# A ResNet-style block and a spatial attention on Trainium2: the end of the work ("drain") written out anew

## The reference, cut to what matters

```
x = x + L0(gn(x))
    # L0: r = relu(sum over 4 groups of lambda * bn2(conv3x3(sign(relu(bn1(conv3x3(sign(v)))))))  + v),  v = gn(x)
x = x + L1(gn(x))
    # L1: mid = v * m                       v = gn(x), m = mask resized to 28x28
    #     atten = sigmoid(conv7x7([mean over channels of mid, max over channels of mid, m]))
    #     out = mid * atten
    #     relu(5 * ((out - mean) * rsqrt(var + eps) * gamma + beta))     mean, var of each image and channel
```

## Time and profile before

| | us |
|---|---|
| median of 3 runs (258.95 to 261.13) | 260.57 |
| the profiled execution | 262.13 |
| its span, first to last instruction | 260.3 |
| PE busy, share of the span | 226.2, 87% |
| DVE | 224.4, 86% |
| ACT | 187.2, 72% |
| POOL | 169.4, 65% |
| mean granted clock of PE | 0.951 |

### The profile page before, as it was taken

One profiled execution on the slowest core, in us unless ns is written; L12 is line 12 of the kernel. 1 busy time (PEld: TensorE's weight loads), 2 busy tenths in 40 slices (PEclk: granted clock), 3 DMA queues, 4 the chain that ended last, 5 costly groups with the idle time before them and its releaser, 6 DMA issues.

```text
span 260.3 us, 7041 instructions
## 1 busy us (share of the span) xinstructions
PE 226.2 (87%) x2693; PEld 145.3 (56%) x2693; DVE 224.4 (86%) x535; ACT 187.2 (72%) x228; POOL 169.4 (65%) x242
## 2 busy tenths in 40 slices
PE   8789887979999999998999999999999998577640
PEld 3356544555666566655665666557565666335630
DVE  4899899899999999999999999999899997565181
ACT  3966777878878987797979897989798863351311
POOL 4458121553526557498958797979697868889842
PEclk9999999999999999999999999999999999779555
DMA  6999604202010602241225122521342044141114
GB/s 201 373 289 400 236 13 125 70 0 64 3 63 16 176 0 64 83 107 65 64 73 178 62 64 74 180 75 56 105 146 95 31 140 152 58 154 62 62 62 185
DMA packets 11975, 28.81 MB, mean 111 GB/s; under 512 B 2230, under 2 KB 3383, under 8 KB 11943
## 3 DMA queue, kind: packets, MB, share of 16 engines
q1 hardware_dynamic: 11797, 28.37, 33.4%
q10 hardware_dynamic: 146, 0.01, 0.0%
HBM read 21.76 MB, written 6.61 MB: 109 GB/s over the span
## 4 chain that ended last, share of the span: by engine, by line
DVE 41%; PE 22%; issue 11%; POOL 10%; DMA 7%; ACT 6%; SPq 1%; POOLq 0%; DVEq 0%
DVE bnst L646 9%; DVE big L702 7%; PE big L1006 6%; PE big L985 6%; DVE RD L725 5%; POOL X L435 4%; DVE acc L733 3%; DVE S L705 3%; PE small L1046 3%; PE big L1079 3%; DVE gate L699 3%; DMA o<-in_w 2%; PE small L1060 2%; POOL o L415 2%; DVE red L755 2%
## 5 line engine op out<-in xcount | busy, mean ns | idle before, releaser
L1006 PE MATMUL big<-S,w2t 64*64 64x392 f16 x1152 | 55.3, 332 | 5.0 <-DVE S L705 4.9
L985 PE MATMUL big<-E,w1t 64*128 64x392 f16 x576 | 54.5, 331 | 1.3 <-DVE w1t L800 1.1
L1006 PEld LDWEIGHTS big<-S,w2t 64*64 64x64 f16 x1152 | 30.7, 106 | 24.7 <-DVE S L705 9.0
L985 PEld LDWEIGHTS big<-E,w1t 64*128 64x128 f16 x576 | 25.5, 94 | 23.6 <-issue 5.4
L1025 PE MATMUL big<-RD,wa 128*64 128x392 f16 x384 | 35.0, 330 | 3.2 <-issue 3.2
L1046 PE MATMUL small<-cs,o 128*112 128x130 f32 x224 | 33.6, 291 | 4.7 <-POOL o L415 2.2
L415 POOL TENSOR_TENSOR o<-o,mask_b 128x784 f32<-128x784 f32 x15 | 27.8, 1853 | 13.0 <-ACT o L569 10.3
L435 POOL TENSOR_TENSOR X<-X,acc 128x784 f32<-128x784 f32 x15 | 27.7, 1849 | 11.6 <-ACT acc L563 11.6
L1046 PEld LDWEIGHTS small<-cs,o 128*112 128x112 f32 x224 | 26.8, 179 | 15.0 <-issue 8.1
L646 DVE BATCH_NORM_STATS2 bnst<-X 128x6 f32<-128x392 f32 x64 | 32.9, 555 | 1.9 <-POOL X L435 1.1
L705 DVE SCALAR_TENSOR_TENSOR S<-big,thr,gate 128x784 f16<-128x784 f32 (+1 forms) x32 | 32.3, 1011 | 1.1
(11 more groups left out here) (130 smaller groups left out, 354.7 us busy)
## 6 DMA issues: line engine op xcount, KB each, us to landing
X<-in_x SPq DMA_DIRECT2D x16, 392.0 KB, 11.8
mask_b<-mask_rows SPq DMA_DIRECT2D x32, 196.0 KB, 4.0
out<-o SPq DMA_DIRECT2D x16, 392.0 KB, 2.4
att_b<-attention_rows SPq DMA_DIRECT2D x28, 196.0 KB, 3.7
o<-in_w SPq DMA_DIRECT2D x3, 576.0 KB, 7.2
o<-in_masks SPq DMA_DIRECT2D x1, 512.0 KB, 10.2
band<-in_band SPq DMA_DIRECT2D x1, 441.0 KB, 9.7
cs<-in_cst SPq DMA_DIRECT2D x1, 399.0 KB, 9.3
```

Of the source, the lines that this page charges most:

```text
L985: mm = pe.matmul(acc[:, LOW + HALF * hh:LOW + HALF * (hh + 1)], w1t[64 * hh:64 * hh + 64, q, s, :], window(RH * hh, s // 3, s % 3, E[64 * ...
L1006: mm = pe.matmul(acc[64 * q:64 * q + 64, LOW + HALF * r:LOW + HALF * (r + 1)], w2t[64 * r:64 * r + 64, s, 64 * q:64 * q + 64], window(RH * ...
```

## The change

The loops of the four engines run to k = 14. Step 15 and the drain are written out:

- The last pair's L0 is finished by halves of 392 columns in PSUM: `mix(15, 0)` stands ahead of `group_2(14)` and `turn(13, 1)`, `mix(15, 1)` behind `turn(13, 2)`; `finish_half` (DVE), `relu_halves` (ACT) and `add_half` (DVE, with its `bn_stats`) work in place in `big1`. `X[:, 15]` is not written, the last sum reads the PSUM.
- `normalise2(15)` is gone. u is made from the sums as (x - mean) * mask by `make_u_part` (DVE, 336 and 448 columns), without 1/sigma. 1/sigma is in the matrix that turns: `make_turn_w` (ACT, 128x130, the identity times r2). The instance norm of pair 15 takes r2 into its variance and scales (`last_pair_scales`, three small POOL operations; `late_eps`).
- The turned chunks of pairs 14 and 15 have six banks of their own (`LAST_BANKS`), `attention(13)` writes `big0`; the spread of pair 15 goes to `big2`, of 14 to `big0`, pair 15 first, each counted by halves, and `attend_last` multiplies and takes statistics by halves.
- The five operations of `scale3` are, from pair 9, split: eps on DVE (`late_eps`), power on POOL (`late_power`, pairs 10 and 11 in one), the three products on ACT (`scale_late`, each with one or two per-partition operands), ahead of the relu (`late_relu`). The order at the end is 15 (by halves), 12, 14, 13. The sums of 15, 12 and 13 are DVE's, of 14 POOL's.
- `repeat_picks` (ACT L580) moves from the drain into step 3 of the loop. `keep_clock` in the drain is 3, 6, 6 and 5 matmuls, where it was 8, 10, 3 and 2. `sigmoid(15)` stands ahead of the relus of pairs 10 to 15. The mask column of pair 15 is made ahead of `make_u(14)`.
- SP stores in the order 9, 10, 11, 15 (two halves), 12, 14, 13, one store more than before.

```diff
+            def finish_half(m):
+                ps = sums("y", m, 1)
+                dve.wait_ge(y_done, 2 * LAST + m + 1)
+                dve.scalar_tensor_tensor(ps, X[:, LAST, half(m)], r1[:, LAST:NT], ps, ALU.mult, ALU.add)\
...
+            def make_u_part(n):
+                dve.scalar_tensor_tensor(o[:, LAST, a:z], sums("y")[:, a:z], nm2[:, LAST:NT], mask_b[:, LAST % 2, a:z],
+                                         ALU.add, ALU.mult).then_inc(u_parts, 1)
...
+            def make_turn_w():
+                act.wait_ge(rstd2, NT)
+                act.activation(turn_w[:, :], cs[:, K_ID:K_ID + P + 2], ACT.Copy, scale=r2[:, LAST:NT])\
...
+            def scale_late(t):
...
+                act.wait_ge(late_pow, nth_pow(t) + 1)
+                act.activation(nsc3[:, one], r3[:, one], ACT.Copy, scale=minus[:, 0:1]).then_inc(scaled_late[t], 1)
+                act.activation(sc3[:, one], r3[:, one], ACT.Copy, scale=plus[:, 0:1]).then_inc(scaled_late[t], 1)
+                act.wait_ge(scaled_late[t], 1)
+                act.activation(bi3[:, one], mv[:, 2, t, 0:1], ACT.Identity, bias=g5[:, 1:2], scale=nsc3[:, one])\
...
 scalar:
+            round_sums2(15, 0); move_back(15, 0); last_relu(8); round_sums2(15, 1); move_back(15, 1)
+            relu_halves(0); normalise2(14); relu_halves(1); late_relu(9); sigmoid(13); make_turn_w(); sigmoid(15)
+            late_relu(10); late_relu(11); late_relu(15, half(0)); late_relu(15, half(1), False); late_relu(12); late_relu(14); late_relu(13)
 gpsimd:
+            add_x(14); attend(10); last_sum(8); power2(14); late_power(9); mask_column(14); mask_column(15)
+            make_u(14); attend(11); power2(15); last_pair_scales(); last_sum(9); attend(12); late_power(10)
+            attend(13); late_power(15); last_sum(10); late_power(12); last_sum(11); late_power(14)
+            late_power(13); sum_14()
 vector:
+            stats_o(9); late_eps(9); split_sums(15, 0); stats_x1(14); reduce_chunks(13, 0); split_sums(15, 1)
+            terms2(14); finish_half(0); reduce_chunks(13, 1); reduce_chunks(13, 2); finish_half(1)
+            add_half(0); add_half(1); add_up(LAST, 1); stats_o(10); terms2(15); make_u_part(0); make_u_part(1)
+            reduce_chunks(14, 0..2); reduce_chunks(15, 0..2); stats_o(11); late_eps(11); attend_last(15)
+            late_eps(15); stats_o(12); late_eps(12); attend_last(14); late_eps(14)
+            late_sum(15, half(0), 1); late_sum(15, half(1), 2); stats_o(13); late_eps(13)
+            late_sum(12, n=3); late_sum(13, n=5)
 tensor:
+            conv2(15, 0); turn(13, 0); conv2(15, 1); mix(15, 0); group_2(14); turn(13, 1); turn(13, 2); mix(15, 1)
+            keep_clock(3, big[0][:, 0:512]); attention(13); keep_clock(6, big[0][:, 512:BIG]); group_2(15)
+            turn(14, 0..2); turn(15, 0..2); pe.wait_ge(pooled, 45); keep_clock(6, big[0][:, 512:BIG])
+            attention(15); keep_clock(5, big[0][:, 512:BIG]); spread_attention(15); spread_attention(14)
-            attention(13); turn(14, 0..2); pe.wait_ge(split, 2 * NT); keep_clock(8, big[2]); group_2(15)
-            keep_clock(10, big[2]); turn(15, 0..2); keep_clock(3, big[2]); attention(15); keep_clock(2, big[2])
-            spread_attention(14); spread_attention(15)
```

More of the change, by code:

```diff
@@ L473, in _ @@
             pool.wait_ge(cleared, CLEARED)
-            for k in range(1, NT):
+            for k in range(1, NT - 1):
                 add_x(k - 1)
@@ L627, in _ @@
                 relu_block(k)
-            last_relu(9)
-            sigmoid(13)
[L631 to L635, removed]
-            sigmoid(15)
-            last_relu(13)
-            last_relu(14)
-            last_relu(15)
+            round_sums2(15, 0)
+            move_back(15, 0)
+            last_relu(8)
+            round_sums2(15, 1)
+            move_back(15, 1)
+            relu_halves(0)
+            normalise2(14)
+            relu_halves(1)
+            late_relu(9)
+            sigmoid(13)
+            make_turn_w()
+            sigmoid(15)
+            late_relu(10)
+            late_relu(11)
+            for m in range(2):
+                late_relu(15, half(m), m == 0)
+            late_relu(12)
+            late_relu(14)
+            late_relu(13)
         @block.vector
@@ L881, in _ @@
             stats_x(2)
-            for k in range(NT):
+            for k in range(NT - 1):
                 stats_o(k - 6)
@@ L1153, in _ @@
             keep_clock(3, big[0][:, 512:BIG])
-            for k in range(NT):
+            for k in range(NT - 1):
                 conv2(k, 0)
-                if has(k + 1):
-                    conv1(k + 1, 0)
+                conv1(k + 1, 0)
                 if k == 0:
@@ L1180, in _ @@
                 join(k + 2)
+            conv2(15, 0)
+            turn(13, 0)
+            conv2(15, 1)
+            mix(15, 0)
+            group_2(14)
+            turn(13, 1)
+            turn(13, 2)
+            mix(15, 1)
+            keep_clock(3, big[0][:, 0:512])
             attention(13)
+            keep_clock(6, big[0][:, 512:BIG])
+            group_2(15)
             for n in range(3):
                 turn(14, n)
-            pe.wait_ge(split, 2 * NT)
-            keep_clock(8, big[2])
-            group_2(15)
-            keep_clock(10, big[2])
             for n in range(3):
                 turn(15, n)
-            keep_clock(3, big[2])
+            pe.wait_ge(pooled, 45)
+            keep_clock(6, big[0][:, 512:BIG])
             attention(15)
-            keep_clock(2, big[2])
-            for t in range(POOL_ATTENDS, NT):
+            keep_clock(5, big[0][:, 512:BIG])
+            for t in (15, 14):
                 spread_attention(t)
```

270 lines of the change are left out of this document (191 added, 79 removed).

## The result

The changed kernel takes 251.23 us at the median of 4 runs (249.67 to 251.84); the kernel before, run beside it, takes 260.85. The ratio is 0.9638, with a 95% interval of 0.9592 to 0.9684: 9.4 us, or 3.6%, faster. Forecast were 248.5, range 245.5 to 252.5. The two profiled executions lie further apart than the medians: spans of 260.3 and 247.9, so 12.4 us. That gap is the first thing to explain. The profiled execution of before, 262.13, stands 1.3 above its median, and that of the changed kernel, 249.67, is the fastest of its four, 1.6 under its median.

The account below looks back on a forecast made before the run. The prediction took VectorE to bound the body and handovers the last 40 us. A drain gain of 12.65 us, less 0.2 and 0.35, gave 12.1; 260.6 - 12.1 = 248.5 us, range 245.5 to 252.5.

Parts of the forecast that it names:

- every sign that the prediction named: Drain: clock 1.0 until 235, turning near 225, attention ending near 230, sigmoid right behind, VectorE without gaps, last sum near 245.
- The 12.1: Whole kernel: the forecast gain in us, 12.65 from the drain less 0.2 for the loop and 0.35 for new handovers.
- rival 1: New drain: the clock falls for 7 us, adding 3.5 us, to 252.0; chance 0.17.
- Halves: Step 15: pair 15 finished in 392-column halves, operations 0.56 to 0.59 us each, second statistics done at 222.4.
- The matrix: Pair 15's group norm: 1/sigma in the turning matrix replaces a 3.7 us path; turning starts at 225.2, 9.0 us earlier.
- `repeat_picks` at 0.2: Loop step 3 on ScalarE: its 1.68 us, moved there, costs 0.2 us, bounds 0 and 1.7.
- The sigmoid "3.5": Behind attention(15): the sigmoid of pair 15 no longer queues behind the relus, so 3.5 us are gone.
- The scales shared by three engines: Last chain: moving the scale operations off GpSimd, 1.9 us before, gives 0.4 us here.
- The last power: Last chain, pair 13: GpSimd's power runs from eps at 241.25 to 241.85.
- the old whole add: Pair 15's front: it took 1.88 us beside GpSimd's multiplication, 0.97 alone, giving 0.9 of the 3.35 us gain.
- Rival 2: End of the drain: GpSimd's powers behind its sums and overlapping sums give back 2 us, to 250.5; chance 0.18.
- Rivals 3 and 4: Drain: 3, all at half clock, 262.5, chance 0.03; 4, only sigmoid and 2 us of idle matmuls gained, 255, chance 0.07.

Follow-up runs that it names:

- e9: The kernel before run once more with nothing edited: ratio 0.9985 to the other runs of the same kernel, drain 45.00 us.
- e3: The changed kernel with the last pair finished whole in PSUM instead of by halves: ratio 0.9679 to the kernel before, drain 37.27 us.
- e4: The changed kernel with pair 15 normalised on ScalarE, masked on VectorE and turned by the identity: ratio 0.9709 to the kernel before, drain 38.67 us.
- e2: The kernel before with only the sigmoid of pair 15 moved ahead of the relus of pairs 11 and 12: ratio 0.9937, drain 43.05 us.
- e5: The changed kernel with the scale products from pair 9 on back on GpSimd instead of ScalarE: ratio 0.9723 to the kernel before, drain 37.24 us.
- e11: The changed kernel with calls reordered on all engines and fewer idle matmuls (3, 2 and 1): ratio 0.9578 to the kernel before, drain 33.68 us.
- e10: The changed kernel with VectorE's last sum of pair 12 waiting for GpSimd's last power: ratio 0.9633 to the kernel before, drain 35.08 us.
- e1: The changed kernel run once more with nothing edited: ratio 0.9644 to the kernel before, drain 34.92 us.
- e7: The changed kernel with GpSimd's sum of pair 8 behind the power of pair 14 and mask columns: ratio 0.9625 to the kernel before, drain 34.66 us.
- e12: The kernel of e11 with the last sums of pairs 11 and 14 moved from GpSimd to VectorE: median 248.24 us, ratio 0.9500 to the kernel before.

## Why the prediction was right, and where it wasn't

**The dates.** Forecast and measured, in the one profile: end of `mix(15, 1)` 219.25 and 219.54; second statistics of pair 15 222.4 and 222.62; variance 224.05 and 224.16; turning of pair 15 225.2 and 225.33; end of `attention(15)` 230.25 and 229.94; eps of pair 13 241.25 and 240.92; last sum 244.9 and 245.09. The method, a date for each handover from durations of rows, holds to 0.35 us over 35 us of drain, and every sign that the prediction named came. Against the profiled execution it said 250.0, and that took 249.67.

**The step that failed** is the last one of the sum: "the median of the runs shown is 1.6 under it, so 260.6 - 12.1 = 248.5". The 12.1 contained 2.3 us that belong to the one execution profiled: the clock had fallen over its idle matmuls and again over its whole spread, and e9, the same kernel, has a drain of 45.0 instead of 47.26. I took the difference in the profile's base and subtracted it from a median in which that loss is only partly there. With e9's drain it is 45.0 - 35.0 = 10 us, 251 from the median; measured are 251.23. The rows had the sign of it: the profiled execution stood above the median, and two slices at 0.7 were read as a risk of the new kernel and not as a loss of the old that a median has only in part. So the number is right partly by luck: 251.23 lies outside the forecast's own 246.5 to 250, and inside the wide range because that was stretched for rival 1, which the profiles of the changed kernel don't show.

**The terms.** Halves: 1.26 by e3; the sum had them only in a date. The matrix: the prediction put the way from the variance to the turning at 3.7 before and 1.15 after, and it took 1.17; e4, which kept the rest of the change, gives 1.9 to the matrix. `repeat_picks` at 0.2: nothing to see. The rounding came late, but VectorE took its result at 73.02 (before 73.24), and step 15 starts at 210.12 (before 210.30); in ten profiles, of the changed kernel and its variants, it starts between 210.0 and 211.7, so 0.2 couldn't be told. The sigmoid "3.5": its place was right, but e2 shows that freed alone it is worth about 2, since GpSimd is next. The scales shared by three engines: I gave them "0.4" and left "the rest of the gain" to the order of the pairs; e5 gives 2.1 to the sharing. Added up, these parts are some 7 of the 10 us. The order of the pairs, the spread by halves and with pair 15 first, and the new places of the mixes and the idle matmuls were not taken out one by one, so how the rest is parted between them is not shown. The last power took 1.21 instead of the 0.6 that I took, which the slack of other terms covered.

**One row misread.** The prediction took the old whole add, 1.88, as running beside GpSimd's multiplication of 2.57. The add started at 222.57, while GpSimd's `make_u(14)` ran from 221.78 to 223.62, and the multiplication started only at 223.57. So `make_u(14)` held the add, and the add, to 224.45, held the multiplication. The price of one overlap was taken as 0.9 from this; in e11 it is 1.4 and 1.3, by how much of the other engine's operation is left when one starts.

**The rivals.** Rival 1, a fall of the clock in the new drain: not in the two profiles of the changed kernel, but in e4's at 217 us, where it cost 1.6 us. In e5 and e10 it fell at 234 us, inside the spread, which took 4.9 instead of 3.82; pair 14's half of it came late by that, and nothing waited for it. The prediction took the loop's rows to speak against a fall without a long gap; e1's windows at 24 to 28 us have one. Rival 2, the end giving some back: not at the changed kernel's end, but it is what e10 and e11 ran into, by the overlap that the prediction named. Rivals 3 and 4: nothing of them.

The contention was told from the earlier trace rows, with the Trainium skill, GPSIMD Engine Reference, Specifications, beside it: GpSimd's and VectorE's shared SBUF interfaces contend when a VectorE instruction has two SBUF inputs. The runs agree and go further: operations on 128x1 elements are held as well. VectorE's took 0.22 in e7 and 1.76 in e3, GpSimd's power 0.55 in e10 and 1.21 without its edit.

## What to carry to other kernels

Date each handover of a drain from the rows, engine by engine and queue by queue; it comes out to a few tenths. But make the sum of a kernel with idle PE against several executions, or take out first what the clock did in the one that was profiled. When an engine is freed from the path, look at once at who is next and how far behind (e2: against e9, 4.5 us on the spread and 1.95 at the end). And keep elementwise work on two SBUF tensors from running on VectorE and GpSimd at the same time: here VectorE doing all of it was faster than both (e12).

## What the runs showed of the hardware that I had not expected

A VectorE operation on 128x1 elements with two SBUF inputs waits until GpSimd's running operation on two 128x784 tensors ends: it took 0.22, 0.70, 0.93 and 1.76 us, and in e3 and in the changed kernel it ended within 0.02 us of GpSimd's.

One SBUF tensor is enough in one form. The eps of pairs 10 and 11, on 128x2 elements, took 0.17 us in the changed kernel's profile and 1.61 in e1, where GpSimd's multiplication had started ahead of it and it ended at 231.83, the multiplication at 231.80; the same operation on 128x1 took 0.15 beside a sum of GpSimd (e1, 236.98, with the sum from 236.34 to 238.18).

```profile
229.96 1.84 POOL L470 TENSOR_TENSOR o<-o,att_b 128x784 f32<-128x784 f32 x1 [1.58 <-DMA att_b<-attention_rows]
```

```profile
230.22 1.61 DVE L781 TENSOR_SCALAR ve<-mv 128x2 f32<-128x2 f32 x1
```

Two large operations side by side behave as one after the other: 2.41 and 2.25 us on VectorE for 0.97, and 2.41 to 2.58 on GpSimd for 1.84. In e11 two sums on each engine took from 239.01 to 244.21, 5.2 us, where one after the other would be 5.6, and VectorE alone did four in 3.65.

And a gap of 1.73 us on PE was followed by the lower clock in one execution (e4), where gaps of 1.47 (e1), 1.68 (e5) and 2.56 (e3) were not.
